# Grouped-query attention in float32: scores as three products of rounded halves instead of one full-precision product

## The reference, cut to what matters

```
q = rope(layernorm(x) @ Wq)      # 32 heads of 128
k = rope(ctx @ Wk); v = ctx @ Wv # 8 heads of 128
s = 30 * tanh((q . k) * 0.0884 / 30); masked; w = softmax(s)
x = x + tanh(g) * (w @ v) @ Wo
```

## Time and profile before

| | us |
|---|---|
| runs | 914.53, 915.41, 923.25 |
| median of the three | 915.41 |
| profiled execution | 916.81 |
| its span, first to last instruction | 915.0 |
| mean granted TensorE clock, as a share | 0.986 |
| PE busy | 874.7 (96% of the span) |
| DVE busy | 607.7 (66%) |
| POOL busy | 417.2 (46%) |
| ACT busy | 326.1 (36%) |

### The profile page before, as it was taken

How to read it: one execution, slowest core, us unless ns; L and a number is a source line. 1 busy time by engine, 2 the same in 40 slices (tenths; PEclk the granted TensorE clock), 3 DMA queues, 4 the chain that set the end, 5 groups by cost and what they waited for, 6 DMA issues and landing times.

```text
span 915.0 us, 13893 instructions
## 1 busy us (share of the span) xinstructions
PE 874.7 (96%) x4778; PEld 711.7 (78%) x4778; DVE 607.7 (66%) x1059; ACT 326.1 (36%) x590; POOL 417.2 (46%) x423
## 2 busy tenths in 40 slices
PE   4999999999999999999999999999999999998993
PEld 4778877977877887887897787778799999557882
DVE  5975575366566517557536657668889887879446
ACT  4424124214114212412421411423256678552330
POOL 4652253153163215235315315334888866828651
PEclk9999999999999999999999999999989999999997
DMA  9020120011011002012001100203255230663448
GB/s 322 21 92 1 35 92 1 12 47 47 18 64 47 14 1 92 1 35 92 1 13 46 47 1 1 82 1 116 51 140 152 69 80 13 254 252 121 161 157 321
DMA packets 42352, 71.17 MB, mean 78 GB/s; under 512 B 7081, under 2 KB 14826, under 8 KB 42098
## 3 DMA queue, kind: packets, MB, share of 16 engines
q1 hardware_dynamic: 37170, 58.00, 19.8%
q0 software_dynamic: 3680, 12.06, 3.9%
q10 hardware_dynamic: 1440, 0.24, 0.1%
HBM read 53.64 MB, written 10.23 MB: 70 GB/s over the span
## 4 chain that ended last, share of the span: by engine, by line
PE 89%; DVE 5%; issue 2%; DMA 1%; ACT 1%; ACTq 1%; DVEq 0%; SPq 0%; POOLq 0%
PE ps L1426 19%; PE ps L1428 19%; PE ps L1427 19%; PE ps L1547 6%; PE ps L1539 6%; PE ps L1676 6%; PE ps L1555 3%; PE ps L1664 3%; PE ps L1657 2%; DVE w_lo L1285 1%; PE ps L1806 1%; PE ps L1746 1%; PE ps L1620 1%; PE ps L1776 1%; PE ps L1632 1%
## 5 line engine op out<-in xcount | busy, mean ns | idle before, releaser
L556 POOL TENSOR_TENSOR q_t<-rot_a,rot_b 128x512 f32<-128x512 f32 x64 | 82.6, 1291 | 152.5 <-DVE rot_b L1012 152.5
L1010 DVE TENSOR_TENSOR rot_a<-ps,cos 128x512 f32<-128x512 f32 x80 | 55.2, 689 | 87.1 <-PE ps L1428 86.5
L1426 PE MATMUL ps<-xt_hi,wq_hi 128*128 128x512 f32 x256 | 107.6, 420 | 0.5 <-DVE rot_b L1012 0.5
L1426 PE MATMUL ps<-wo_hi,at_hi 128*128 128x512 f32 x256 | 106.8, 417 | 0.4 <-DVE at_lo L1120 0.4
L1428 PE MATMUL ps<-xt_hi,wq_lo 128*128 128x512 f32 x256 | 101.2, 395 | 0.0
L1427 PE MATMUL ps<-xt_lo,wq_hi 128*128 128x512 f32 x256 | 101.0, 395 | 0.0
L792 ACT ACTIVATE ps<-ps 128x512 f32<-128x512 f32 x64 | 37.2, 582 | 178.6 <-PE ps L1539 178.6
L1428 PE MATMUL ps<-wo_hi,at_lo 128*128 128x512 f32 x256 | 100.3, 392 | 0.0
L1427 PE MATMUL ps<-wo_lo,at_hi 128*128 128x512 f32 x256 | 99.9, 390 | 0.0
L805 ACT ACTIVATE at_hi<-ps 128x512 fp32r<-128x512 f32 x64 | 38.2, 597 | 171.7 <-PE ps L1555 171.7
L1125 DVE TENSOR_TENSOR X<-ps,X 128x512 f32<-128x512 f32 x64 | 44.2, 690 | 74.5 <-PE ps L1428 74.2
(11 more groups left out here) (223 smaller groups left out, 2103.3 us busy)
## 6 DMA issues: line engine op xcount, KB each, us to landing
wq_raw<-in_wq SPq DMA_DIRECT2D x8, 1024.0 KB, 5.4
wo_raw<-in_wo SPq DMA_DIRECT2D x8, 1024.0 KB, 5.2
w_raw<-in_we SPq DMA_DIRECT2D x8, 1024.0 KB, 7.1
X<-in_x SPq DMA_DIRECT2D x4, 512.0 KB, 12.3
wk_raw<-in_wk SPq DMA_DIRECT2D x8, 256.0 KB, 2.9
q_t<-in_ctx_t SPq DMA_DIRECT2D x2, 1024.0 KB, 9.3
wv_raw<-in_wv SPq DMA_DIRECT2D x4, 512.0 KB, 4.3
ctx_s<-in_ctx SPq DMA_DIRECT2D x8, 256.0 KB, 3.0
```

The source lines that it names most:

```text
L556: nc.gpsimd.tensor_tensor(dst, rot_a[:, r % 2, :], rot_b[:, r % 2, :], ALU.add).then_inc(rope_ok, 1)
L1010: nc.vector.tensor_tensor(heads(rot_a[:, r % 2, :]), heads(bank), bcast(cos[:, :], 4), ALU.mult)
L1426: nc.tensor.matmul(dst, w_hi, x_hi, start=start and k == 0, stop=False)
```

## The change: what it does

- The rotated query and key tiles are split too. GpSimd's sum still writes `q_t` or `k_t` in float32; ScalarE then makes `q_hi`, `k_hi` (`turned_hi`, ten of 512 columns a group), and the lo part is made in place over the float32 tile: by VectorE for r = 0 to 5 (`turned_lo`, six a group), by GpSimd for r = 6 to 9 (four a group).
- `scores` is a `product`: three matmuls in place of one float32 matmul. `scores(0)` waits for VectorE's six lo parts, `scores(4)` for GpSimd's four.
- VectorE makes the lo part of tile r-1 right behind the rotation of tile r (r = 3 to 6); those of the key tiles come behind the last `add` of the group before.
- GpSimd makes the lo parts of wo behind the sums of r = 5, 6 and 7 (one, one, two) and no longer behind those of r = 2 to 5; ScalarE makes their hi parts between the hi parts of the query tiles. The hi parts of r = 8 and 9 stand on ScalarE between `weights(2)` and `at_hi` of batch 0, and between `weights(3)` and `at_hi` of batch 1.
- The raw wo shares its memory with its lo part. Its load therefore waits for all eight outputs of the group before, and stands behind the load of wq on SyncE's queue.
- `v_ones` has a row of P + 2 and not P + 4 floats, and one semaphore (`tri_ok`) is merged into another (`kz_ok`), with its counts adapted.

The core of the diff:

```
-        wo_raw = sb("wo_raw", [P, G, D])
         wo_hi = sb("wo_hi", [P, G, D], F32R)
+        wo_raw = over("wo_raw", [P, G, D])
         wo_lo = sb("wo_lo", [P, G, D], F32R)
-        q_t = sb("q_t", [P, G, N])
+        q_hi = sb("q_hi", [P, G, N], F32R)
+        q_t = over("q_t", [P, G, N])
+        q_lo = sb("q_lo", [P, G, N], F32R)
...
@@ sync
-                sp.wait_ge(wo_lo_ok, CREDIT + G * g)
-                load_wo(g)
                 sp.wait_ge(qp_mm, CREDIT + 8 * g)
                 load_wq(g)
+                sp.wait_ge(wo_mm, CREDIT + B * g)
+                load_wo(g)
@@ gpsimd
+            def turned_lo(g, r):
+                gp.wait_ge(sh_ok, CREDIT + 10 * g + r + 1)
+                lo_part(turned_tile(r, q_lo, k_lo), turned_tile(r, q_t, k_t), turned_tile(r, q_hi, k_hi), sl2_ok)
             def group(g, p, odd, last=False):
-                for r in range(2, 10):
+                for r in range(2, 8):
                     rope_sum(g, r)
-                    if r < 2 + G:
-                        wo_split(g, r - 2)
+                    if r >= 5:
+                        wo_split(g, r - 5)
+                wo_split(g, 3)
+                rope_sum(g, 8)
+                turned_lo(g, 6)
+                turned_lo(g, 7)
+                turned_lo(g, 8)
+                rope_sum(g, 9)
+                turned_lo(g, 9)
@@ scalar
+            def turned_hi(g, r):
+                ac.wait_ge(rope_ok, CREDIT + 10 * g + r + 1)
+                hi_part(turned_tile(r, q_hi, k_hi), turned_tile(r, q_t, k_t), sh_ok)
             def group(g, p, odd, last=False, first=False):
-                for k in range(G):
-                    wo_split(g, k)
...
+                for k in range(G):
+                    turned_hi(g, 2 + k)
+                    wo_split(g, k)
+                turned_hi(g, 6)
                 weights(0)
                 weights(1)
+                turned_hi(g, 7)
                 for b in range(B):
                     if b + 2 < B:
                         weights(b + 2)
+                    if b < 2:
+                        turned_hi(g, 8 + b)
...
+                if not last:
+                    turned_hi(g + 1, 0)
+                    turned_hi(g + 1, 1)
@@ vector
+            def turned_lo(g, r):
+                ve.wait_ge(sh_ok, CREDIT + 10 * g + r + 1)
+                nc.vector.tensor_tensor(turned_tile(r, q_lo, k_lo), turned_tile(r, q_t, k_t), turned_tile(r, q_hi, k_hi).bitcast(F32),
+                                        ALU.subtract).then_inc(sl_ok, 1)
...
+            turned_lo(0, 0)
+            turned_lo(0, 1)
...
-                for r in range(2, 8):
+                rotate(g, 2)
+                for r in range(3, 8):
                     rotate(g, r)
+                    if r < 7:
+                        turned_lo(g, r - 1)
...
                 add(B - 1)
+                if not last:
+                    turned_lo(g + 1, 0)
+                    turned_lo(g + 1, 1)
@@ tensor
                 def scores(b):
-                    if b in (0, 4):
-                        pe.wait_ge(rope_ok, CREDIT + 10 * g + 6 + b)
+                    if b == 0:
+                        pe.wait_ge(sl_ok, CREDIT + 6 * g + 6)
+                    if b == 4:
+                        pe.wait_ge(sl2_ok, CREDIT + 4 * g + 4)
                     pe.wait_ge(e_ok, CREDIT + B * g + b - 1)
-                    nc.tensor.matmul(ps[:, 2 + b % 2, :], k_t[:, b * P:(b + 1) * P], q_t[:, :, b * P:(b + 1) * P],
-                                     start=True, stop=True).then_inc(s_mm, 1)
+                    rows = slice(b * P, (b + 1) * P)
+                    product(ps[:, 2 + b % 2, :], [(k_hi[:, rows], k_lo[:, rows], q_hi[:, :, rows], q_lo[:, :, rows])]).then_inc(s_mm, 1)
```

More of the change, by code:

```diff
@@ L143, in flamingo_gated_two_layers @@
         at_2 = place[0]
-        wo_raw = sb("wo_raw", [P, G, D])
         wo_hi = sb("wo_hi", [P, G, D], F32R)
+        wo_raw = over("wo_raw", [P, G, D])
         wo_lo = sb("wo_lo", [P, G, D], F32R)
-        q_t = sb("q_t", [P, G, N])
-        k_t = sb("k_t", [P, N])
-        v_ones = sb("v_ones", [P, B, 2, P + 4])
+        q_hi = sb("q_hi", [P, G, N], F32R)
+        q_t = over("q_t", [P, G, N])
+        q_lo = sb("q_lo", [P, G, N], F32R)
+        k_hi = sb("k_hi", [P, N], F32R)
+        k_t = over("k_t", [P, N])
+        k_lo = sb("k_lo", [P, N], F32R)
+        v_ones = sb("v_ones", [P, B, 2, P + 2])
         e_w = sb("e_w", [P, 2, G * P])
@@ L290, in flamingo_gated_two_layers @@
         kp_mm, vp_mm, qp_mm, rot_ok, rope_ok, v_ok = sem("kp_mm"), sem("vp_mm"), sem("qp_mm"), sem("rot_ok"), sem("rope_ok"), sem("v_ok")
+        sh_ok, sl_ok, sl2_ok = sem("sh_ok"), sem("sl_ok"), sem("sl2_ok")
         s_mm, th_ok, ex_ok, e_ok = sem("s_mm"), sem("th_ok"), sem("ex_ok"), sem("e_ok")
@@ L310, in flamingo_gated_two_layers @@
         we_in = [sem(f"we_in{e}") for e in range(EX)]
-        be_in, route_in, tri_ok, hrow_out = sem("be_in"), sem("route_in"), sem("tri_ok"), sem("hrow_out")
+        be_in, route_in, hrow_out = sem("be_in"), sem("route_in"), sem("hrow_out")
         wel_v, rank_mm, slot_ok, hot_ok, list_mm = (sem("wel_v"), sem("rank_mm"), sem("slot_ok"), sem("hot_ok"),
@@ L345, in gate_bank, with turned_tile @@
             return ps[:, 6, b * EX:(b + 1) * EX] if b < EARLY else ps[:, 7, (b - EARLY) * EX:(b - EARLY + 1) * EX]
+        def turned_tile(r, queries, keys):
+            if r < 2:
+                return keys[:, r * HALF:(r + 1) * HALF]
+            half, head = divmod(r - 2, G)
+            return queries[:, head, half * HALF:(half + 1) * HALF]
         def bcast(t, n):
@@ L512, in _ @@
         def _(gp):
-            start_counts(gp, (ones_ok, eps_ok, rstd_ok, wkl_ok, wvl_ok, wql_ok, wo_lo_ok, rope_ok, wbl_ok, x2_ok, kz_ok,
+            start_counts(gp, (sl2_ok, ones_ok, eps_ok, rstd_ok, wkl_ok, wvl_ok, wql_ok, wo_lo_ok, rope_ok, wbl_ok, x2_ok, kz_ok,
                               va_ok, kb_ok, qkl_ok, om_ok, wel_ok))
@@ L550, in rope_sum @@
                 gp.wait_ge(rot_ok, CREDIT + 10 * g + r + 1)
[L551 to L556, removed]
+                nc.gpsimd.tensor_tensor(turned_tile(r, q_t, k_t), rot_a[:, r % 2, :], rot_b[:, r % 2, :], ALU.add).then_inc(rope_ok, 1)
+            def turned_lo(g, r):
+                gp.wait_ge(sh_ok, CREDIT + 10 * g + r + 1)
+                lo_part(turned_tile(r, q_lo, k_lo), turned_tile(r, q_t, k_t), turned_tile(r, q_hi, k_hi), sl2_ok)
             def group(g, p, odd, last=False):
-                for r in range(2, 10):
+                for r in range(2, 8):
                     rope_sum(g, r)
-                    if r < 2 + G:
-                        wo_split(g, r - 2)
+                    if r >= 5:
[7 more added lines that the diff above has]
+                turned_lo(g, 9)
                 if last:
@@ L715, in _ @@
                 ac.dma_start(dst, src).then_inc(consts_in, 16)
-            start_counts(ac, (ot_ev, gates_ok, hth_ok, cth_ok, wkh_ok, wvh_ok, wqh_ok, wo_hi_ok, v_ok, th_ok, ex_ok, ah_ok, wbh_ok,
-                              lge_ok, zt_ok, qkh_ok, p_ok, pt_ok, gelu_ok, weh_ok, r_ok, gh_ok, tri_ok))
+            start_counts(ac, (sh_ok, ot_ev, gates_ok, hth_ok, cth_ok, wkh_ok, wvh_ok, wqh_ok, wo_hi_ok, v_ok, th_ok, ex_ok, ah_ok, wbh_ok,
+                              lge_ok, zt_ok, qkh_ok, p_ok, pt_ok, gelu_ok, weh_ok, r_ok, gh_ok))
             def hi_part(dst, raw, done):
@@ L779, in _ @@
             row_hi_first(7)
+            turned_hi(0, 0)
+            turned_hi(0, 1)
             def group(g, p, odd, last=False, first=False):
-                for k in range(G):
-                    wo_split(g, k)
                 if not odd and not first:
@@ L927, in _ @@
             ac.wait_ge(route_in, 32)
-            nc.scalar.activation(tri[:, :], tri_raw[:, :], ACT.Copy).then_inc(tri_ok, 1)
+            nc.scalar.activation(tri[:, :], tri_raw[:, :], ACT.Copy).then_inc(kz_ok, 1)
             ac.wait_ge(c2_mm, CREDIT + B)
@@ L1367, in _ @@
             nc.vector.scalar_tensor_tensor(scatter_i[:, at], listed[:, at], -1.0, padding[:, at], ALU.add, ALU.add).then_inc(slot_ok, 1)
-            ve.wait_ge(kz_ok, CREDIT + 2)
+            ve.wait_ge(kz_ok, CREDIT + 3)
             nc.vector.tensor_tensor(t_upto[:, :], t_before[:, :], t_e[:, :], ALU.add).then_inc(slot_ok, 1)
@@ L1779, in chosen @@
                 return nc.tensor.matmul(ps[:, 0, 0:EX], ones_r[:, :], sel[:, b, :], start=b == 0, stop=b == B - 1)
-            pe.wait_ge(kz_ok, CREDIT + 1)
-            pe.wait_ge(tri_ok, CREDIT + 1)
+            pe.wait_ge(kz_ok, CREDIT + 2)
             pe.wait_ge(sel_ok, CREDIT + 1)
```

2 lines of the change are left out of this document (1 added, 1 removed).

## The result

The changed kernel takes **927.13 us** (median of 15 runs, 923.27 to 932.42) against 916.29 (median of 15, 912.59 to 923.25): a ratio of 1.011 [1.0087, 1.0133], 10.8 us or 1.1% slower. The forecast was 971, with 920 to 985 around it. The sign was right and the size was not. What happened is the mechanism of case B (VectorE gets in first), to which I gave 0.14; its time of 922 is 5 too low, and that it came so near is in part luck, as the last part shows.

What follows compares the result with a forecast made beforehand. TensorE, 89% of the chain, was taken to bound the kernel, with VectorE nearly full in the query tiles. Eight groups at 5.5 us (44), 1.4 before the loop and 10 for the clock gave +55.4, 971 us; range 920 to 985.

Steps and rivals of the forecast that it cites:

- case B: Behind the rotations VectorE's lo parts get in ahead of GpSimd's sums: +6.3 us in all, 922 us; chance 0.14.
- VectorE's lo parts behind the rotations: In the query tiles each lo part waits out GpSimd's sum, 1.93 us (other end 0.69); 5.2 us lost a group.
- the row of 2.10: Earlier-trace lo part of the experts on VectorE, begun before GpSimd's at 828.67, taking 2.10 us; used as price evidence.
- The clock: Some 3 us of TensorE idle ahead of `scores(0)` lowers the granted clock, 1.7 us each, six of eight groups: 10 us.
- `scores(0)` in case B: First score of a group starts at 14.19 and not 13.87, waiting for lo(5): 0.3 us lost a group.
- covered by two tiles: GpSimd's lo parts of wo end at 25.0, `output(0)` stands past 27 behind two query tiles: priced at nothing.
- the chain at `scores(4)`: Last sum, hi(9), lo(9) in sequence make `scores(4)` start 1.19 us late, less its own 0.17: 1.0 lost a group.
- the savings at scores 0 to 2: The first three scores, between query tiles, save 0.17 us each in full: 0.5 us a group.
- 5 to 7: `scores(5)` to `scores(7)` save only 0.07 us each because the output waits for `at_lo`: 0.2 us a group.
- the 1.4 ahead of the loop: Before the loop VectorE's two key lo parts, 0.69 us each, delay a rotation TensorE waits for: 1.4 us, once.
- TensorE's products at 0.23 a matmul: A score as three matmuls at 0.23 us takes 0.69 against 0.86 in float32, at unchanged pace.
- A: VectorE's lo parts wait out GpSimd's sums behind the rotations: 971 us, own range 955 to 990; chance 0.71.

Runs made afterwards that it cites:

- ts_lo: Changed kernel with VectorE's lo part replaced by a TENSOR_SCALAR of one SBUF tile, lo parts left out; 956.72 us, 1.0428 to the kernel before.
- late2: Changed kernel with three small reciprocals on VectorE between each rotation of r = 3 to 6 and the lo part behind it; 971.94 us, 1.0616 to the kernel before.

## Why the prediction was wrong, by its own steps

**VectorE's lo parts behind the rotations: the step that failed.** I put 1.93 us on each, from the earlier trace rows and the row of 2.10 in the earlier trace rows, and kept 0.69 as the other end. Measured: 0.69 in 24, 0.88 in 8. Neither row was the situation. The one in the earlier trace rows is a TENSOR_SCALAR, which loses from the same start (ts_lo), and the same trace held one that did not lose, at 24.66, which I did not use. In the other, 828.67 to 830.77, GpSimd was already busy with a gather (an indirect DMA that it issues) when VectorE began, as the timeline of GpSimd shows, before:

```profile
827.92 0.97 POOL L677 DMA_INDIRECT rows_in<-h_rows,gather_i  x1 [0.31 <-issue]
```

But a gather alone does not keep VectorE waiting: the 0.69 at 817.03 lies inside another one, before:

```profile
816.91 0.95 POOL L677 DMA_INDIRECT rows_in<-h_rows,gather_i  x1 [0.30 <-issue]
```

And a busy GpSimd alone does not: the eight lo parts that began inside a part of wo (after) still went ahead of the next sum, for 0.88. So the 2.10 stays unexplained, and with it four more rows of that stage (2.30 to 2.32), which also began inside a gather, 0.44 to 0.45 ahead of GpSimd's subtraction, and lost. They are no case of VectorE first on an idle GpSimd, which is what the change has. The traces stay 47.4 us below my sum (55.4 less 8.0). On this price hung 36.6 of them (41.6 less 5.0), on the next step 10.

**The clock** fell nowhere in the attention after the change: my forecast of it rested on 3 us of idle time ahead of `scores(0)`, and only 0.3 to 0.5 came. Where they did come (late2), five groups showed falls, one of them twice as long as the row I had taken; in sum the groups lost 10.2 us to it (0.5 us windows, each by what its clock lacks to 1.00), close to the 10 of six falls at 1.7. Idle time alone does not settle it: the 1.99 us at 44.43 (after) had no fall behind it, 1.98 at the same place in late2 had one.

**`scores(0)` in case B** was put at 0.3 a group and came to 0.6. The lo part behind the wo part (0.2) was not in it; it is the wo part of GpSimd that I held to be covered by two tiles, and whose cover I priced for TensorE alone. The remaining 0.1 is not traced.

**Right, by number:** the chain at `scores(4)` (1.0 a group), the savings at scores 0 to 2 (0.5) and 5 to 7 (0.2, because of `at_lo`), and the 1.4 ahead of the loop. Also right: TensorE's products at 0.23 a matmul.

**Missing:** the pace of the output matmuls, from moved buffers, +2.3; and the stall at the turn of the loop, -4.0. I had quoted that stall only as a source for the clock. Case B's sum of +6.3 plus both, the extra 0.3 a group and 0.9 behind the attention is 6.3 + 2.3 + 2.4 - 4.0 + 0.9 = 7.9, the 8.0 of the profiles. So B's +6.3 came near by luck: what it lacked nearly cancels, and the -4.0 has nothing to do with scores. The medians differ by 10.8, and the interval of the ratio, times 916.29, is 8.0 to 12.2. Part of what lies above 8.0 goes with the granted clock: the 71 runs of the kernel before in the experiments' comparisons have a median of 0.989, the changed kernel's 15 runs 0.987, and at equal clock the mean spans differ by 7.2 to 9.3 us. Whether the lower clock belongs to the change or to chance, the runs don't show.

**The chances.** I gave A 0.71 on two rows that spoke for it, and wrote of B that VectorE had begun first in both. The rule of the Trainium skill ("SBUF — State Buffer", "SBUF: two separate sides") made B the likeliest, and I set it aside for rows of another kind or state. The traces agree with it for the instruction that the change adds, behind a rotation (0.69 when first, 1.65 when second). Before setting aside a rule that rows contradict, ask whether those rows are its case.

## What to carry to other kernels

Price an instruction by a row of the same kind, the same operands and the same state of its rival engine; where only another kind is there, keep both ends as likely. When tiles take new places or a program grows, look for the pace of the untouched matmuls and for stalls at a loop's turn: each was worth 2 to 5 us here, about as much as the change itself. A matmul's saving counts only where no chain of other engines ends at the same place, and moving a chain's last link to a faster engine helped here only in small part until the slower one was kept off SBUF meanwhile.

## What the runs showed of the hardware

- Who waits when VectorE and GpSimd meet on SBUF depends on the order of starts and on the kind of VectorE's instruction: a subtraction of two tiles that starts 0.02 to 0.05 us ahead of a sum on GpSimd keeps its 0.69 (the sum takes 1.80); 0.17 behind, it takes 1.65. A TENSOR_SCALAR of one tile 0.04 ahead takes 1.62, and one 0.38 ahead kept its 0.54. Five subtractions that began inside a gather, 0.24 to 0.45 ahead of a subtraction on GpSimd, lost (2.10 to 2.32), for a reason that no run shows.
- A shift of 128 bytes between stationary and moving tile changes the pace of products of 512 columns: 233 to 227 ns for query tiles, 232 to 228 for outputs, both where the shift makes the remainders of 256 bytes equal. Key tiles have equal remainders and run at 231 to 232, so the remainder is not the whole rule.
- A program can hold a stall of 2 us on issue behind the turn of TensorE's loop in each of three profiles (1.96, 2.11, 2.19) and lose it when 37 instructions are put ahead (2.8 to 4.0 us). With the stall go nine more packets on the DMA queue named "instruction".
